# Branch-one attention scores: two heads side by side in the array, and the maximum pass moved next to the exponential pass

## The reference, cut to what matters

```
branch one:  q, k, v = xn @ W + b          # 16 heads of 8 columns
             scores  = q @ k.T / 8**0.5, causal
             y1      = softmax(scores) @ v, then @ Wm + bm
branch two:  x2 = xn + attention(rmsnorm(xn))   # 16 heads of 64 columns, shared rotary keys, causal
             y2 = x2 + shared expert + top 2 of 8 experts of rmsnorm(x2)
out        = x + y1 + y2
```

## Time and profile before

| what | value |
|---|---|
| median of the runs | 1463.7 us |
| profiled execution | 1464.32 us |
| its span (first to last instruction) | 1462.3 us |
| granted TensorE clock, mean | 0.978 |
| TensorE matmul busy | 1376.2 us, 94% |
| VectorE busy | 1146.6 us, 78% |
| ScalarE busy | 997.3 us, 68% |
| GpSimd busy | 587.5 us, 40% |

### The profile page before, as it was taken

How to read it: one execution, slowest core, us unless ns; L and a number is a source line. 1 busy time by engine, 2 the same in 40 slices (tenths; PEclk the granted TensorE clock), 3 DMA queues, 4 the chain that set the end, 5 groups by cost and what they waited for, 6 DMA issues and landing times.

```text
span 1462.3 us, 36231 instructions
## 1 busy us (share of the span) xinstructions
PE 1376.2 (94%) x14438; PEld 1073.2 (73%) x14438; DVE 1146.6 (78%) x2358; ACT 997.3 (68%) x1585; POOL 587.5 (40%) x610
## 2 busy tenths in 40 slices
PE   4689999999999999999999999999999999999985
PEld 3467777777877777787777777777777777777653
DVE  7877797978879797987979788797879879787613
ACT  2156777767777777777777777777776777777762
POOL 5323434354433434443343445334344534433112
PEclk9589999999999999999999999999999999999997
DMA  6666655645465565556556545655655465555100
GB/s 161 122 124 122 122 118 108 129 100 115 85 129 116 115 120 107 115 91 118 115 114 119 112 110 96 112 120 113 116 114 113 102 101 119 116 106 115 17 3 14
DMA packets 136677, 155.86 MB, mean 107 GB/s; under 512 B 32687, under 2 KB 126543, under 8 KB 127391
## 3 DMA queue, kind: packets, MB, share of 16 engines
q1 hardware_dynamic: 118078, 151.97, 51.5%
q10 hardware_dynamic: 18432, 1.58, 1.6%
HBM read 82.79 MB, written 67.11 MB: 103 GB/s over the span
## 4 chain that ended last, share of the span: by engine, by line
PE 69%; DVE 18%; ACT 8%; issue 4%; POOL 0%; DMA 0%; ACTq 0%; DVEq 0%
PE ps L217 22%; PE psm L217 16%; PE pse L217 15%; PE psv L217 10%; DVE R L734 5%; ACT PT L1100 3%; DVE rt L796 2%; PE ps L325 2%; ACT pse L1106 2%; DVE th L846 1%; PE ps L391 1%; DVE xs L662 1%; ACT th L1179 1%; DVE th L858 1%; ACT th L1148 1%
## 5 line engine op out<-in xcount | busy, mean ns | idle before, releaser
L734 DVE TRANSPOSE_TENSOR_REDUCE R<-psm 128x32 f32<-128x1024 f32 x384 | 478.7, 1247 | 133.3 <-PE psm L217 132.2
L1100 ACT ACTIVATE PT<-pse 128x1024 f32<-128x1024 f32 x384 | 392.3, 1022 | 210.4 <-PE pse L217 210.3
L1106 ACT ACTIVATE pse<-maskb 128x512 f32<-128x512 bf16 x510 | 285.4, 592 | 16.9 <-ACT PT L1100 6.2
L217 PE MATMUL pse<-qsB,ks 98*128 98x512 f32 x768 | 215.0, 402 | 8.0 <-ACT pse L1106 7.8
L1296 POOL TENSOR_TENSOR ts_<-ts_,pA 128x512 f32<-128x512 f32 x32 | 37.2, 1162 | 445.8 <-DVE pA L668 445.8
L217 PE MATMUL psm<-qsB,ks 96*128 96x512 f32 x512 | 180.6, 414 | 6.0 <-DVE R L734 6.0
L217 PEld LDWEIGHTS pse<-qsB,ks 98*128 98x128 f32 x768 | 137.1, 189 | 58.6 <-issue 18.9
L1304 POOL TENSOR_TENSOR tc_<-tc_,ts_ 128x512 f32<-128x512 f32 x64 | 82.3, 1286 | 190.4 <-DVE ts_ L688 190.4
L217 PE MATMUL pse<-qsA,ksA 98*128 98x128 bf16 x1536 | 127.0, 220 | 9.7 <-ACT pse L1106 8.4
L217 PEld LDWEIGHTS psm<-qsA,ksA 96*128 96x128 bf16 x1536 | 96.3, 100 | 51.9 <-issue 27.7
L217 PE MATMUL psm<-qsA,ksA 96*128 96x128 bf16 x1536 | 120.9, 223 | 13.3 <-DVE R L734 12.6
(11 more groups left out here) (194 smaller groups left out, 2623.7 us busy)
## 6 DMA issues: line engine op xcount, KB each, us to landing
scrB<-pB SPq DMA_DIRECT2D x32, 1536.0 KB, 6.0
qsB<-scrB SPq DMA_DIRECT2D x384, 128.0 KB
scrA<-pA SPq DMA_DIRECT2D x32, 384.0 KB, 2.8
qsA<-scrA SPq DMA_DIRECT2D x186, 64.0 KB
ksA<-scrA SPq DMA_DIRECT2D x186, 64.0 KB
xs<-in_x SPq DMA_DIRECT2D x16, 256.0 KB, 9.0
out<-zz SPq DMA_DIRECT2D x16, 256.0 KB, 4.7
qsB<-same SPq DMA_DIRECT2D x64, 16.0 KB
```

The lines of the kernel that those rows point to most:

```text
L217: return e.matmul(o, l, r, start=start, stop=stop, skip_group_check=True)
L734: e.tensor_reduce(red, MX[:].rearrange("p i (c q) -> p (i c) q", q=32), AX.X, ALU.max, apply_transpose=True).then_inc(s_mr, 1)
L1100: e.activation(PT[g % 4], EX[:], ACT.Exp, scale=(8.0 ** -0.5, 0.125)[br]).then_inc(s_pt, 1)
L1106: e.activation(EX[:, i].rearrange("p (h q) -> p h q", h=4), bc(maskb[:], 4), ACT.Copy).then_inc(s_sd, 1)
```

## The change

The eight heads of a pass are taken in pairs: one in rows 0 to 63 of the array, one in rows 64 to 127. `qsA` and `ksA` have 128 partitions and half as many heads in the free dimension, and no zero rows in the contraction. The maximum pass has its masks in front, and stands directly before the exponential pass of its slot. The exponential pass of branch one waits for both mask copies at once. The weights' columns are reordered on the host accordingly.

```diff
-        qsA = [sb(f"qsA{i}", [98, H, S], BF16) for i in range(2)]
-        ksA = [sb(f"ksA{i}", [98, H, S], BF16) for i in range(2)]
+        qsA = [sb(f"qsA{i}", [128, H // 2, S], BF16) for i in range(2)]
+        ksA = [sb(f"ksA{i}", [128, H // 2, S], BF16) for i in range(2)]
@@ TensorE
+            def pair_scores(b, bk, u, K, start):
+                s = b % 2
+                kt, qt, h0 = UNITS[u]
+                keys, queries = slice(128 * kt, 128 * kt + 128), slice(128 * qt, 128 * qt + 128)
+                for j in range(4):
+                    for i in range(2):
+                        rows = slice(64 * i, 64 * i + K)
+                        t = mm(bk[:, i, 128 * j:128 * j + 128], ksA[s][rows, h0 // 2 + j, keys], qsA[s][rows, h0 // 2 + j, queries],
+                               start and j == 0, True)
                 return t
@@ max_unit
-                    for i in range(2):
-                        t = scores(br, b, MX, u, i, 96, True)
-                    if UNITS[u][0] == UNITS[u][1]:
+                    diagonal = UNITS[u][0] == UNITS[u][1]
+                    if diagonal:
                         for i in range(2):
-                            t = mask(MX, i, False)
+                            mask(MX, i, True)
+                    t = pair_scores(b, MX, u, 48, not diagonal)
@@ exp_unit
+                if br == 0:
                     if diagonal and g:
-                        w.wait_ge(s_sd, 2 * seeds(g) - 1 + i)
-                    t = scores(br, b, EX, u, i, 98, not diagonal)
+                        w.wait_ge(s_sd, 2 * seeds(g))
+                    t = pair_scores(b, EX, u, 50, not diagonal)
@@ TensorE's loop, ahead of the first group of tasks
-                    if n1 < NB:
+                    if n1 < NB and br:
                         max_unit(br, n1, u)
@@ TensorE's loop, behind the first group of tasks
                     now += 0.5
+                    if n1 < NB and not br:
+                        max_unit(br, n1, u)
                     if body:
                         exp_unit(br, c, u)
@@ ScalarE, max_row
-                for r in range(2):
-                    dst, src = (qsA, qsB)[br][s][96 + r:97 + r, :, :], (cA, cB)[br][:, r]
...
+                for r in range(2):
+                    if br == 0:
+                        for i in range(2):
+                            dst = qsA[s][64 * i + 48 + r:64 * i + 49 + r, :, :].rearrange("o h (b c) -> o (h b) c", c=32)
+                            e.dma_start(dst, cA[64 * i:64 * i + 64, r]).then_inc(d_c[0], 16)
...
@@ set-up: memset of ksA on VectorE, of ones on ScalarE, of qsA on GpSimd go; GpSimd, ahead of stats(0):
+            def setup_ones(i):
+                for n, r in enumerate((32, 96)):
+                    e.memset(ksA[i][r:r + 32], 1.0).then_inc(s_k1, 1)
+                    w.wait_ge(s_k1, 2 * i + n + 1)
@@ SyncE, stack_a: 4 writes and 16 reads for an image (32 reads for image 0)
-                e.dma_start(scrA[s].rearrange("x q p t -> p (x q) t"), pA[:].rearrange("p x q t -> p (x q) t")).then_inc(d_aw[s], 16)
+                for i in range(2):
+                    for q in range(2):
+                        e.dma_start(scrA[s][q, i].rearrange("(x d) h t -> (d h) x t", x=3), pA[64 * i:64 * i + 64, :, q]).then_inc(d_aw[s], 16)
...
+                for h, n, done in ((0, 8, d_ar[s]),) if b else ((0, 4, d_a0), (4, 4, d_ar[0])):
+                    for i in range(2):
+                        for q, dst in ((0, qsA[s]), (1, ksA[s])):
+                            for r, x, m in RUNS[q]:
+                                e.dma_start(dst[64 * i + 8 * r:64 * i + 8 * (r + m), h:h + n, :],
+                                            scrA[s][q, i, 8 * x:8 * (x + m), h:h + n, :]).then_inc(done, 16)
```

More of the change, by code:

```diff
@@ L129, in build @@
         sq, dT = th[0], th[1]
-        scrA = [nc.dram_tensor(f"scrA{i}", (3, 2, 128, S), BF16).ap() for i in range(2)]
+        scrA = [nc.dram_tensor(f"scrA{i}", (2, 2, 24, 8, S), BF16).ap() for i in range(2)]
         scrB = [nc.dram_tensor(f"scrB{i}", (12, 128, S), F32).ap() for i in range(2)]
@@ L158, in build @@
         s_dd, s_ee, s_cm, s_th, s_h = (sem(n) for n in ("s_dd", "s_ee", "s_cm", "s_th", "s_h"))
[L160 to L161 removed]
+        s_half, s_k1, s_ksi, s_wa, s_wn, s_wb, s_sa, s_sb = (
+            sem(n) for n in ("s_half", "s_k1", "s_ksi", "s_wa", "s_wn", "s_wb", "s_sa", "s_sb"))
         s_bv = sem("s_bv")
@@ L226, in mask, with scores @@
                 return mm(bk[:, i].rearrange("p (h q) -> p h q", h=4), identb[:], bc(maskb[:], 4), start, True)
-            def scores(br, b, bk, u, i, K, start):
+            def scores(b, bk, u, i, K, start):
                 s = b % 2
@@ L231, in scores @@
                 keys, queries = slice(128 * kt, 128 * kt + 128), slice(128 * qt, 128 * qt + 128)
[L232 to L240, removed]
+                o = bk[:, i].rearrange("p (h q) -> p h q", h=4)
+                r = qsB[s][0:K, h0 + 4 * i:h0 + 4 * i + 4, queries]
+                mm(o, ks1[s][0:K, keys], r, start, False)
+                return mm(o, ks2[s][0:K, keys], r, False, True)
+            def pair_scores(b, bk, u, K, start):
[7 more added lines that the diff above has]
+                               start and j == 0, True)
                 return t
@@ L287, in exp_unit @@
                     w.wait_ge(s_pt, g)
-                w.wait_ge(d_c[br], 32 * (b + 1))
+                w.wait_ge(d_c[br], (64, 32)[br] * (b + 1))
                 diagonal = UNITS[u][0] == UNITS[u][1]
-                for i in range(2):
+                if br == 0:
                     if diagonal and g:
-                        w.wait_ge(s_sd, 2 * seeds(g) - 1 + i)
-                    t = scores(br, b, EX, u, i, 98, not diagonal)
+                        w.wait_ge(s_sd, 2 * seeds(g))
+                    t = pair_scores(b, EX, u, 50, not diagonal)
+                else:
+                    for i in range(2):
+                        if diagonal:
+                            w.wait_ge(s_sd, 2 * seeds(g) - 1 + i)
+                        t = scores(b, EX, u, i, 98, not diagonal)
                 t.then_inc(s_ex, 1)
@@ L875, in setup_stack @@
             def setup_stack(i):
-                e.memset(ksA[i][:], 0.0).then_inc(s_zk, 1)
                 e.memset(ks1[i][96:98, :].bitcast(F32), 1.0)
@@ L1216, in _ @@
                         prep_nope(n2)
-                    if c == -1 and k == 4:
-                        setup_stack(1)
                     if k == 6 and odd and moe:
@@ L1340, in _ @@
             stats2(1)
-            e.memset(qsA[0][:], 0.0).then_inc(s_zq, 1)
             prep_r0(0)
@@ L1347, in _ @@
             prep_rlo(0)
-            e.memset(qsA[1][:], 0.0).then_inc(s_zq, 1)
             for c in range(-1, NB + 3):
@@ L1402, in stack_a @@
                 if b >= 2:
[L1403 to L1405 removed]
+                    w.wait_ge(d_ar[s], 256 * (b // 2))
+                for i in range(2):
+                    for q in range(2):
+                        e.dma_start(scrA[s][q, i].rearrange("(x d) h t -> (d h) x t", x=3), pA[64 * i:64 * i + 64, :, q]).then_inc(d_aw[s], 16)
+                w.wait_ge(d_aw[s], 64 * (b // 2 + 1))
                 if b >= 2:
                     w.wait_ge(s_ex, unit(0, b - 2, 5) + 1)
[L1408 to L1414 removed]
+                w.wait_ge(s_k1, 2 * s + 2)
+                for h, n, done in ((0, 8, d_ar[s]),) if b else ((0, 4, d_a0), (4, 4, d_ar[0])):
+                    for i in range(2):
+                        for q, dst in ((0, qsA[s]), (1, ksA[s])):
+                            for r, x, m in RUNS[q]:
+                                e.dma_start(dst[64 * i + 8 * r:64 * i + 8 * (r + m), h:h + n, :],
+                                            scrA[s][q, i, 8 * x:8 * (x + m), h:h + n, :]).then_inc(done, 16)
             def stack_b(b):
```

36 lines of the change are left out of this document (13 added, 23 removed).

## The result

Four runs of the changed kernel gave 1542.51 to 1560.94 us, median 1552.24; the kernel before, beside it on the same chip, 1464.05. The ratio is 1.060, 95% interval 1.053 to 1.067. The forecast of 1512 had the sign right and was 40 us short, outside its range. The profiled execution of the changed kernel took 1560.94 us (span 1559.1), the slowest of the four, against 1464.3 (span 1462.3) before: 96.8 us between the spans.

The account below looks back on a forecast made before the run. TensorE busy 94%, but VectorE limits the odd branch-one half (18.32 of 19.60 us). Odd c 35.7, even c 2.0, c = 1 and 2 1, queue 9, start 1: +48.7 on 1464.3, 1513, median 1512; range 1482 to 1536.

Parts of the forecast that it names:

- odd c, wait: Odd branch-one half: TensorE idles for `prep_xlo`, VectorE for slot 2's pass; +2.55 us each, 35.7 in all.
- even c: Even c: `moe_d` matmuls cover most of VectorE's work, ahead and behind cancel; +0.15 us each, between -1.2 and +1.5.
- ScalarE's queue: Slot 7: four DMAs issued instead of two, ahead of the mask copies; +0.3 us an image, between 0 and 0.6.
- start: Start: `qsA[1]` and VectorE memsets go, four half-size memsets, DMA issues and low-clock passes come; +1 us, between -4 and +5.
- rest of images 0 to 2: c = 1 and 2, which have fewer tasks: +1 us.
- end: c = 30 and 31: 0 us.
- It idles until 711.43, 2.5 us: Slot 1, odd c: behind the exponential pass TensorE has nothing in front of `tail_in` and waits 2.5 us for `prep_xlo`.
- +1.0 if 64 descriptors cost as much as 128: Slot 7, ScalarE's queue: upper case for issuing four DMAs; +0.2 if 64 descriptors cost nearly nothing.
- Pairs overlap: Branch-one passes: pairs run at once, 0.22 us a pass for 0.45; 2.7 us less a half, 1.2 for changing division.
- The rule of the Trainium skill: Tiling speeds up TensorE, not the emptying of PSUM; VectorE's 18.32 of 19.60 us in the odd branch-one half agrees.
- TensorE's saving: Rival: VectorE's waits are absorbed and 1.5 us a half arrive; 1418 us, or 1420 with VectorE's limit; chance 6%.
- the rival of 1535: Rival: pairs do not overlap; odd c +0.44, even c +1.3, 23 us more, 1535 us; chance 10%.

Follow-up runs that it names:

- wait filled: Changed kernel with ten unread 512-column matmuls into `psv` in slot 1 of odd c, in TensorE's wait: 1539.67 us, ratio 1.052.
- order alone: Kernel before, with only the maximum pass of branch one moved behind the slot's first group of tasks: 1525.07 us, ratio 1.042.
- two DMAs: Changed kernel with the rows of the maxima of branch one written by two DMAs of 128 descriptors in place of four: 1531.08 us, ratio 1.046.
- SyncE alone: Changed kernel with only SyncE's part undone: one scratch write per image and 16 reads for image 0, for four and 32: 1559.68 us, ratio 1.064.
- memsets later: Changed kernel with GpSimd's four memsets moved behind its first powers and the first low part of the rotation: 1553.33 us, ratio 1.063.
- cut to 0.85 us: Changed kernel with `norm` and `prep_xlo` ahead of slot 1's reduction on VectorE: 1514.13 us, ratio 1.034.
- pass in front: Changed kernel with the maximum pass of branch one at the head of its slot again: 1501.87 us, ratio 1.026.
- four costs undone: Changed kernel with maximum pass in front, two DMAs, memsets later, and SyncE's one scratch write per image and 16 reads for image 0: 1465.08 us, ratio 1.0014.

## Why the prediction was wrong in size

The profiled execution's difference against the forecast's own sum:

| term | forecast | measured | from |
|---|---|---|---|
| odd c, wait | 14 x 2.55 = 35.7 | 14 x (21.8 - 19.67) = 29.8 | halves without half clock, and wait filled |
| even c | 13 x 0.15 = 2.0 | 13 x 0.29 = 3.8 | table |
| ScalarE's queue | 29 x 0.3 = 9 | 13 x 1.11 + 14 x 0.16 + 4.0 = 20.6 | even halves at full clock 23.12; images 0 to 2 |
| half clock | none | 14 x 1.48 + 7 x 0.79 = 26.2 | halves with and without it |
| start | 1 | 7.3 | table |
| rest of images 0 to 2 | 1 | 3.5 | branch-one halves |
| end | 0 | 5.6 | table |
| sum | 48.7 | 96.8, as between the spans | |

*TensorE's wait in odd c: right.* The exponential pass, the 2.0 to 2.7 us of idle time released by `prep_xlo`, VectorE's idle time ahead of slot 2 and a half of 22 us were all forecast, and at full clock the half is 21.8. The order alone gave a wait of 2.10 us as well.

*"It idles until 711.43, 2.5 us": the step that failed.* The forecast took the wait at its length. In the profiled executions a wait of 2.1 to 2.3 us came with a stretch at 1.2 GHz in all 14 odd halves of the changed kernel, in 13 of 14 with two DMAs, 10 of 14 with SyncE alone, 4 of 14 with the memsets later and 3 of 14 with the order alone; with the wait filled or cut to 0.85 us, or the pass in front, no odd half held any. The clock before was 1.00 in all four halves, and the forecast took it as given. This term is missing from the sum altogether. Its 26 us are over half of the 48 by which the sum fell short of the profiled execution, which was the slowest of the four; in the median run, 9 us shorter and not traced, it will be less.

*ScalarE's queue: right mechanism, mis-sized.* "+1.0 if 64 descriptors cost as much as 128" was the true branch (2.44 for 1.13 us: +1.3). I took 0.3, reasoning that the exponential passes had 0.5 to 1.1 us of slack. In odd c that held (+0.16); in even c the branch-two half grew by 1.1 us at full clock, the added issue time nearly whole, where the forecast allowed 0.6 at most, and in images 0 to 2 the branch-two halves grew by 4.0 together. With two DMAs the branch-two halves are back at 21.97 and 22.08 us and the median is 21 us lower; some of that is half clock, which the even ones then lack.

*Start: mis-sized.* The memsets took 7.36 us, forecast 7; but more of the start showed (7.3 for 1). Branch two's first scratch write came 5.2 us later (39.41 for 34.20), 2.3 of it by the memsets (37.08 with them later) and 2.9 by SyncE's queue, which had 11 more issues for image 0 (36.49 with SyncE's part undone). Undone, the memsets gave back 1.9 us; SyncE's part was 4 us in the last kernel and nothing by itself, so a clean split of the start stays open.

*End: put at nothing.* Images 30 and 31 cost 5.6 us more. With two DMAs, the order alone or SyncE alone the end is back at about 120, with the memsets later it is not; the cause stays open.

*Pairs overlap: right.* 0.24 us forecast 0.22. Side by side, two passes take 399.39 - 398.83 = 0.56 us to the next task (memsets later, c = 7) and 0.09 for the change ahead, in place of 0.90: 0.25 a slot, 1.5 a half. The forecast's 1.5 had another make-up: 2.7 from the overlap less 1.2 for the changes. Apart, as in the pass-in-front kernel, they gain 0.03 each. So the gain needs the two passes together, and both orders that put them together made an engine wait: whether the saving would reach the time without such a wait is not shown.

*The rule of the Trainium skill weighed in the forecast* ("TensorEngine Tiling (Array Packing)", Performance Considerations: tiling does not speed up the emptying of PSUM) fits the kernel with four costs undone: in its odd half TensorE is busy 0.46 us less than before (18.96 for 19.42), VectorE as long as before (18.22 for 18.32), and the half is 0.16 shorter. With the two passes apart the pairs save TensorE so little that no run here puts the rule to a full test.

*The rivals.* TensorE's saving did not arrive. Pairs do overlap, so the rival of 1535 fell by its cause, though its time was nearer.

Which waits bring the clock down, and which of them do not, is not settled: the same 2.32 us did and did not, within one execution.

## What to carry to other kernels

Where a clock of 1.00 stands in the rows of before, price a new TensorE wait at its length and again with a stretch at 1.2 GHz behind it (here 2.2 us and 1.5 more), and put that in the range. Ask of a pass that is moved not how long it is but which engine's list stands behind its reader, and what TensorE has to do meanwhile; undo a change part by part with its halves in a table, since an order that saves 38 us beside one neighbour costs 64 beside another. On an engine that computes, count a DMA by the issue (0.6 us here), not by its bytes.

## What the runs showed of the hardware that I had not expected

- Ten matmuls whose result nobody reads, put into a wait, gave a median 12.6 us lower (1539.67 for 1552.24), and kept all 14 odd halves at full clock.
- The changed kernel's four runs spread over 18 us, and the four of before over 1 us. The stretches at 1.2 GHz differ from one execution to the next: 71.7 us in the profiled execution of 1560.94 us, 20.5 in one of 1541.91 of the kernel with the memsets later.
- Entering and leaving two row groups costs 0.18 us a pass (0.09 before, 0.09 behind), two fifths of the 0.45 us that the pass took before.
- An issue on ScalarE's queue took 0.57 us with 128 descriptors and 0.61 with 64.
- A VectorE copy of two columns that began just behind a GpSimd memset of 1.8 us ended 0.03 us behind it, 1.82 us long for 0.17.
